# A graph network kernel: a block's second half combined right behind its mean, ScalarE's transfers issued later in a slot

## What is computed

```python
h = relu(layernorm(x))
z = h
for l in range(2):
    weights = softmax(z @ envW[l] + envb[l])                # (N, 4)
    agg = segment_mean(z[col], row, N)                      # mean over a node's edges
    combined = concatenate([agg, z], axis=-1)               # (N, 512)
    outputs = einsum('nd,kdo->nko', combined, W[l]) + z[:, None, :]
    z = relu(einsum('nk,nko->no', weights, outputs))
return x + z
```

## Time and profile before

| what | value |
|---|---|
| median of 3 runs | 1765.87 us (1763.92 to 1765.96) |
| the profiled execution | 1765.67 us, span 1763.5 us |
| TensorE (PE) matmul busy | 1565.8 us, 89% |
| GpSimd (POOL) | 1180.8 us, 67% |
| VectorE (DVE) | 886.8 us, 50% |
| ScalarE (ACT) | 573.3 us, 33% |
| mean granted TensorE clock | 0.981 |
| DMA | 393.34 MB, mean 223 GB/s |

### The profile page before, as it was taken

One profiled execution on the slowest core, in us unless ns is written; L12 is line 12 of the kernel. 1 busy time (PEld: TensorE's weight loads), 2 busy tenths in 40 slices (PEclk: granted clock), 3 DMA queues, 4 the chain that ended last, 5 costly groups with the idle time before them and its releaser, 6 DMA issues. The chain is left out here.

```text
span 1763.5 us, 35980 instructions
## 1 busy us (share of the span) xinstructions
PE 1565.8 (89%) x8502; PEld 1108.8 (63%) x8503; DVE 886.8 (50%) x2029; ACT 573.3 (33%) x1254; POOL 1180.8 (67%) x1187
## 2 busy tenths in 40 slices
PE   1158999999999999999990899999999999999998
PEld 1036776667767777666760666676667666666665
DVE  6674665666666666566650233433433343433433
ACT  4413444444344434444340122222222222222222
POOL 1377777777777777777745776666667666666663
PEclk9989999999999999999995899999999999999999
DMA  7877777776777777767759887777777777777774
GB/s 216 278 230 222 227 226 217 214 206 205 215 215 224 213 215 224 216 209 212 204 175 381 305 246 213 214 220 213 216 228 227 214 219 220 220 221 212 223 218 146
DMA packets 160202, 393.34 MB, mean 223 GB/s; under 512 B 36989, under 2 KB 61080, under 8 KB 160180
## 3 DMA queue, kind: packets, MB, share of 16 engines
q0 software_dynamic: 92544, 302.70, 58.1%
q10 hardware_dynamic: 35112, 61.46, 9.8%
q1 hardware_dynamic: 32524, 28.91, 5.3%
HBM read 347.61 MB, written 45.37 MB: 223 GB/s over the span
## 5 line engine op out<-in xcount | busy, mean ns | idle before, releaser
L713 POOL DMA_INDIRECT ring<-zp_dram,gather_idx x1152 | 1162.7, 1009 | 492.9 <-issue 280.6
L1367 PE MATMUL agg_ps<-zp,stage 128*128 128x258 f32 x1568 | 447.3, 322 | 24.1 <-PEq L101 24.1
L1400 PE MATMUL mix_ps<-w_sb,turned_z 128*128 128x512 f32 x784 | 400.3, 610 | 33.2 <-PEq L101 30.9
L1329 PE MATMUL agg_ps<-ring,onehot 128*128 x1248 | 386.9, 338 | 18.6 <-PEq L101 13.7
L1400 PE MATMUL mix_ps<-w_sb,turned_m 128*128 128x512 f32 x784 | 392.5, 600 | 1.9 <-PEq L101 0.7
L1369 PE MATMUL agg_ps<-zp,stage 128*128 128x256 f32 x1568 | 384.6, 281 | 0.0
L1107 ACT ACTIVATE stage<-counts_sb 128x512 fp32r<-128x512 uint8 (+1 forms) x416 | 247.1, 605 | 388.3 <-ACTq L101 386.6
L1367 PEld LDWEIGHTS agg_ps<-zp,stage 128*128 128x128 f32 x1568 | 296.1, 189 | 88.1 <-issue 84.3
L1334 PE MATMUL agg_ps<-ring,onehot 128*128 x1248 | 320.6, 285 | 0.0
L1369 PEld LDWEIGHTS agg_ps<-zp,stage 128*128 128x128 f32 x1568 | 296.4, 189 | 34.5 <-issue 34.5
L1329 PEld LDWEIGHTS agg_ps<-ring,onehot 128*128 128x128 f32 x1248 | 238.1, 191 | 67.0 <-issue 61.7
(11 more groups left out here) (159 smaller groups left out, 897.9 us busy)
## 6 DMA issues: line engine op xcount, KB each, us to landing
ring<-zp_dram,gather_idx POOLq DMA_INDIRECT x1152, 3.8
zp_dram<-zp SPq DMA_DIRECT2D x7, 1792.0 KB, 7.1
a_dram<-counts_sb ACTq DMA_DIRECT2D x16, 784.0 KB, 5.0
zp_dram<-parts ACTq DMA_DIRECT2D x49, 256.0 KB
zp<-zp_dram SPq DMA_DIRECT2D x4, 1792.0 KB, 19.6
counts_sb<-a_dram ACTq DMA_DIRECT2D x17, 400.0 KB
parts<-in_x ACTq DMA_DIRECT2D x48, 128.0 KB
counts_sb<-a_dram ACTq DMA_DIRECT2D x16, 384.0 KB
```

Of the source, the lines that this page charges most:

```text
L713: pool.indirect_dma_start(out=ring[:, k, t, 0:2 * D].bitcast(F32), out_offset=None, in_=zp_dram[l], in_offset=bass.IndirectOffsetOnAxis(ap ...
L1329: mm = pe.matmul(agg_ps[:, bank, 0:D + 2], onehot[:, place, t, :], rows[:, :, D:2 * D + 2], start=place == 0 and t == 0, stop=True, skip_g ...
L1367: pe.matmul(agg_ps[:, bank, 0:D + 2], stage[:, g % 2, i, :], zp[:, c, D:2 * D + 2], start=c == 0, stop=True, skip_group_check=True)
L1400: mm = pe.matmul(mix_ps[i][:, :], (turned_z, turned_m)[what][:, c, :], w[:, i * HALF:(i + 1) * HALF], start=what == 0 and c == 0, stop=wha ...
```

## The change

On VectorE, `compare_first` of the next sparse block moves from between the mean and the second half in the first slot (k = 0) to the dense slot, behind the logits. The plan's bounds of that block are read once for it, not once for each part. On ScalarE in layer 2, `fetch_x` and `load_counts` no longer open a slot: in the first slot x is fetched behind the mean's copy and the counts are loaded behind the scaling; in the rest slot the finish of the block before, the x load and the counts load stand behind the scaling; in the dense slot the finish of the block before and the x load stand between fills 2 and 3. The wait for the last out store is a step of its own (`free_result`), placed later. In layer 1, the store of the counts stands behind fills 0 and 1. On PE in layer 1, window pairs 3 and 4 of the first slot stand one product earlier, and the first slot no longer reads the dense block's number in either layer.

```diff
@@ VectorE
-                    def compare_first(blk):
-                        lo, _ = units_of(dve, blk)
+                    def compare_first(blk, lo):
...
                                 elif k == DENSE_AT:
                                     following = sparse_block(dve, r, k + 1)
+                                    lo, hi = units_of(dve, following)
+                                    compare_first(following, lo)
                                     dn1 = dense_no(dve, r + 1)
-                                    compare_next(following, 0)
+                                    compare_next(lo, hi, 0)
                                 take_weights()
                                 if k == DENSE_AT:
-                                    compare_next(following, 1)
-                                    compare_next(following, 2)
+                                    compare_next(lo, hi, 1)
+                                    compare_next(lo, hi, 2)
...
                                 take_mean(l, block_of(dve, r, dn, k + 1), bank_of(k))
...
-                                if k < PER_ROUND and k != DENSE_AT:
-                                    compare_first(sparse_block(dve, r, k + 2 if k < DENSE_AT else k + 1))
-                                elif k == PER_ROUND:
+                                if k == PER_ROUND:
@@ ScalarE
                     def scale_z(l):
                         take(act, s_wts)
                         nc.scalar.activation(mix[:], z_in[:], ACT.Copy, scale=wts[:, K:K + 1]).then_inc(s_zs, 1)
-                        if l == L - 1:
-                            take(act, s_out, 16)
-                            act.sem_inc(s_ofree, 1)
+
+                    def free_result():
+                        take(act, s_out, 16)
+                        act.sem_inc(s_ofree, 1)
...
                                 blk = block_of(act, r, dn, k)
-                                if not first:
-                                    fetch_x(blk)
-                                    if k in GROUP_AT:
-                                        load_counts(dn1 if k > DENSE_AT else dn, GROUP_AT[k])
                                 if k == 0:
                                     copy_mean()
+                                    if not first:
+                                        fetch_x(blk)
                                     exps()
                                     scale_z(l)
+                                    if not first:
+                                        load_counts(dn, 1)
+                                        free_result()
...
-                                        store_counts(dn)
                                     else:
                                         take(act, s_ald, PER_ROUND * 16)
                                     for g in range(2):
                                         fill_stage(g)
+                                    if first:
+                                        store_counts(dn)
                                 elif k == DENSE_AT:
-                                    for g in range(2, 4):
-                                        fill_stage(g)
+                                    fill_stage(2)
+                                    if not first:
+                                        finish(l, block_of(act, r, dn, k - 1))
+                                        fetch_x(blk)
+                                    fill_stage(3)
                                     copy_mean()
...
                                     scale_z(l)
+                                    if not first:
+                                        free_result()
...
                                     copy_mean()
                                     exps()
                                     scale_z(l)
+                                    finish(l, block_of(act, r, dn, k - 1))
+                                    fetch_x(blk)
+                                    load_counts(dn1, 0)
                                     copy_z()
+                                    free_result()
                                 begin(l)
-                                if not first:
+                                if not first and k == PER_ROUND:
                                     finish(l, blk)
@@ PE
-                    def first_slot(l, r, dn):
+                    def first_slot(l, r):
...
                         turn_z()
+                        pair(3)
                         product(6).then_inc(s_agg, 1)
-                        pair(3)
+                        pair(4)
                         product(7)
-                        pair(4)
                         pair(5)
...
                         with pe.Fori(0, rounds) as r:
-                            dn = dense_no(pe, r)
-                            first_slot(l, r, dn)
-                            head = dense_slot(l, r, dn)
+                            first_slot(l, r)
+                            head = dense_slot(l, r)
```

15 lines of the change are left out of this document (8 added, 7 removed).

## The result

The changed kernel takes **1716.16 us** (median of 4 runs, 1715.55 to 1718.74) against 1765.91 before in the same series: ratio 0.9723, 95% interval 0.9709 to 0.9738, some 49.7 us less. The forecast was 1708.9, in a range of 1698.5 to 1736, with 1699 to 1717 as its nearer bounds; the result lies at their upper edge. The profiled execution has a span of 1714.3 us, 49.2 less than before.

What follows compares the result with a forecast made beforehand. TensorE (PE), busy 89% of the span, was taken as the bound, the gain being its standstill: 1765.67 - 43.2 (layer 2) - 12.0 (layer 1 dense) - 3.2 (read) + 1.6 (counts) = 1708.9 us, range 1698.5 to 1736.

Steps and rivals of the forecast that it cites:

- Layer 2's rest slot: Exponential no longer waits behind store and load issues, starting 1.5 us sooner; PE's lost 0.2 us a round is regained.
- the floor of 8.9: Layer 1's rest slot of 10.39 us less seven window pairs, taken as layer 2's rest slot without PE stops.
- Layer 2's first slot: PE gets z_in and the bank in time at the slot's start; 1.1 us a round gained.
- Rival B: First slot keeps its stops, by VectorE's chain or PE's sequencer; fills alone help: 1734.5 us, chance 0.15.
- Layer 2's dense slot: Fill 2 ahead of the finish, and an earlier result, remove PE's stop at group 2: 1.4 us a round.
- The counts load: Layer 2's first slot: load moved behind exponential and scaling costs 0.1 us a round, bounds 0 to 1.2; 1.6 in all.
- rival A: Layer 2's dense slot: counts arrive late, fill 0 waits, 1.2 us a round instead of 0.1: 1726.5 us, chance 0.15.
- Layer 1's dense slot: Counts' store behind the fills (0.6) and pairs 3 and 4 earlier (0.15) save 0.75 us a round, 12.0 in all.
- The dropped read: PE's first slots, both layers: no table read saves 0.1 us in 32 rounds, 3.2 in all; at most 9.6.
- Rival D: No difference in time, because another engine, GpSimd with its gathers, would set the pace; chance 0.04.
- Rival C: Slower: unit 0's one-hots in the dense slot come after PE in both layers, 1789 us if 3.2 late; chance 0.04.

Runs made afterwards that it cites:

- b_scalar: The kernel before with only ScalarE's layer 2 order (issues behind the scaling, fill 2 ahead of the finish, free_result apart): 1725.0 us, ratio 0.978.
- b_vector: The kernel before with only VectorE's order (second half right behind the mean, unit 0's one-hots behind the logits): 1744.6 us, ratio 0.988.
- b_layer1: The kernel before with only layer 1's edits (counts' store behind fills 0 and 1, pairs 3 and 4 one product sooner): 1753.0 us, ratio 0.993.
- a_read_back: The changed kernel with TensorE's table read at the head of each round put back: 1713.7 us, ratio to before 0.971.
- a_small_keys: The changed kernel with VectorE's layer 1 window compares cut to two windows each (dense sums not the reference's): 1701.4 us, ratio to before 0.963.
- b_no_read: The kernel before with only TensorE's read of the dense block's number dropped: 1756.1 us, ratio 0.995.

## Why the prediction was right or wrong

**Layer 2's rest slot.** Forecast 0.2 a round, measured 0.60. Mechanism right (b_scalar gives all of it); the floor of 8.9 from layer 1 was 0.4 too high, and what layer 1's rest slot holds beyond its seven pairs stays open.

**Layer 2's first slot.** Forecast 1.1 and the read's 0.1; measured 1.47. b_scalar alone has 0.95 of it. With the read put back the changed kernel keeps 0.69 (14.08 to 13.39), so there the read is worth 0.78, where alone it was worth nothing. The size was near, but the read's share of it was not foreseen. Rival B is out.

**Layer 2's dense slot.** Forecast 1.4, less 0.1 for the counts. The 1.4 was right in size (b_vector 1.33), but I gave it to fill 2's new place, and VectorE's part alone is enough for it. Measured together: 0.45.

**The counts load** is the term that was mis-sized, 0.1 for a measured 0.87 (24.34 to 23.47), 14 us in all where 1.6 stood; the bounds, 0 to 1.2, held it. The step that failed: "the chain is 1.5 us sooner and two issues of about 1.0 us no longer stand ahead of the exponential, so the scaling starts near 1325.5". Counted from the start of the rest slot (1309.02 before, 1374.27 after), the scaling was to come 2.5 us sooner and came 1.8 sooner, at 17.2 us instead of 19.0. The chain, by the issue of the out store, was only 1.2 sooner (14.2 to 13.0), and only one of the two issues is gone from ahead of the exponential: the x load still stands there, 0.4 more between the mean's copy and the scaling. So the load went out at 17.4 us, where the forecast had 16.6 and the kernel before 17.1: 0.3 later and not 0.5 sooner. PE's need moved up by 1.9 (the dense slot starts at 21.1 instead of 23.0), not by 1.3 to 1.7. With the 1.1 us that fill 0 had in hand that makes 1.1 for this round; its stop is 0.9. The load took as long as before, 5.28 for 5.29 us to fill 0 in the two rounds shown, and 3.4 to 5.6 over the rounds of the changed kernel. The Trainium skill's rule to issue a DMA early and wait late ("DMA: Bandwidth & Descriptors", Rules for kernel authors) was right at this place, and I gave it 0.15 as rival A. The same page's fit for transfers issued by GpSimd (Anatomy of one DMA), an estimated 2.9 us for this load, which ScalarE issues, does not hold beside the gather stream; by it there would have been no stop.

**Layer 1's dense slot.** Forecast 0.75, measured 0.73; b_layer1 12.1 us for 12.0.

**The dropped read.** Forecast 0.1 in each of 32 rounds, with an upper bound of 0.3, the duration of the load. Measured alone: 0.65 in layer 1's rounds and 0 in layer 2's; with the way cleared 16.9 us, beyond the bound of 9.6. The bound was wrong, since the read is more than its load. What line 671 runs on PE's sequencer in one round of before:

```profile
L671 PEldq TENSOR_LOAD <-plan x1: 298/298/298, 474.3 to 474.3; - x1
L671 PEldq FUSED_REGOPS  x1: 157/157/157, 474.6 to 474.6; - x1
L671 PEldq SEQ_ASSERT  x1: 24/24/24, 474.8 to 474.8; - x1
```

Together 0.48 us, with the pauses between them more.

**The change of layers** had no term. It cost 9.6 us, the largest miss. The stretch from the last slot of layer 1 to the first dense slot of layer 2 is 81 us, 5% of the span, and I had looked at rounds only. It is also where the end of layer 1 is decided by GpSimd: its last gather of layer 1 ended at 909.4 before and 900.1 after, 9.3 sooner, where PE was 19.6 sooner, and the reload follows the gather. In a_read_back the last gather ends at 894.2, ahead of PE's last logits (900.1) as before the change, and the change of layers is 82.4. Why the gathers end sooner there, beside a slower PE, stays open.

**Rival D** was dismissed from one row of layer 2, where GpSimd had stood 4.26 us. In the stretch 500 to 870 of layer 1 its longest wait was 2.4 us before and is 0.3 after. **Rival C** did not show: in layer 2 PE has no wait but the 13 at a group, and in layer 1 no wait in a dense slot.

Against the sum: 43.2 forecast for layer 2's slots, 16 x 0.60 + 15 x 1.47 + 16 x 0.45 = 38.8 measured, with the counts and the read's part in layer 2; 12.0 for layer 1's dense slots, 11.7; 3.2 for the read, 15 x 0.51 = 7.7 in layer 1 alone; -1.6 for the counts, within the 38.8; nothing for the change of layers, -9.6. The forecast was 7 us too low, and the change of layers is more than the whole of it: the misses on the other terms nearly cancel. That is luck: by slot the forecast had 3.2, 17.6 and 20.8 for layer 2's rest, first and dense slots (the last with the counts), and 9.6, 22.1 and 7.2 were measured.

## What to carry to other kernels

When the bound engine is freed in its loop, list what it runs into at the loop's ends as well: transfers that another engine's list issues behind work of its own do not come sooner because the loop does. Parts that remove the same stop do not add, and a part worth nothing today (the read) can be worth 17 us once the next stops are gone, so it is priced together with them. Before a rival engine is dismissed, its longest wait is to be read in every stage, not in one round.

## What the runs showed of the hardware

**Long compares on VectorE lengthen gathers on GpSimd.** In a first slot of layer 1 of the change, VectorE, then GpSimd:

```profile
471.79 2.19 DVE L937 TENSOR_TENSOR win_key<-key,key_w 128x1960 bf16<-128x1960 f16 x1
```

```profile
471.27 1.41 POOL L712 DMA_INDIRECT ring<-zp_dram,gather_idx  x1 [0.30 <-PE agg_ps L1346]
472.99 1.81 POOL L712 DMA_INDIRECT ring<-zp_dram,gather_idx  x1 [0.30 <-issue]
475.10 0.95 POOL L712 DMA_INDIRECT ring<-zp_dram,gather_idx  x1 [0.30 <-issue]
```

A gather beside the compare takes 1.81 us, the next one 0.95. a_small_keys shows it as cause: shorter compares, 968 ns on average for 1112, at the same number of gathers. It is not a matter of two-byte data alone: in layer 2, where all compares are of fp32 data, the change's gathers beside one-hot compares take 1.06 us on average (stretch 1050 to 1600, 85 of them), those beside no VectorE instruction 0.95 (112). The Trainium skill ("DMA: Bandwidth & Descriptors", SWDGE vs HWDGE vs iDMA) says that the descriptor rings which GpSimd writes are in the memory that VectorE can lock it out of in a two-port mode. No run here shows that mode: the window compares take 1.04 ns an element (1172 ns for 980 elements, 2702 for 2450), as the fp32 ones do (421 ns for 256, 688 for 512), and in which way a compare holds up a gather stays open.

**A table read on TensorE's sequencer is felt some 3 us behind it**, and at 0.65 us a round, twice its load's 0.30 (b_no_read). **A wait that has long been signalled still costs its place in the list:** without SyncE's loop of 16 pairs the reload was issued 5.1 us behind the last gather's end instead of 11.8.
